# Issuing the causal-mask products of two neighbouring diagonal pieces together, in a fused attention and expert kernel on one Trainium2 core

## What is computed

```python
q_lr = jnp.einsum('bhtd,hdr->bhtr', q, Wq_lsr)
k_lr = jnp.einsum('bhtd,hdr->bhtr', k, Wk_lsr)
scores = jnp.einsum('bhir,bhjr->bhij', q_lr, k_lr) * scale
causal_mask = jnp.triu(jnp.ones((Tq, Tq), dtype=bool), k=1)
scores = jnp.where(causal_mask, jnp.float32(-jnp.inf), scores)
attn = jax.nn.softmax(scores, axis=-1)
y = jnp.einsum('bhij,bhjd->bhid', attn, v)
```

## Time and profile before

| | us |
|---|---|
| median of 3 runs | 4045.71 |
| lowest and highest run | 4045.3, 4045.78 |
| span of the profiled execution | 4045.2 |
| PE busy in it | 3714.7 |
| DVE busy in it | 2261.6 |
| ACT busy in it | 1476.5 |
| attention, from the first slot's first score to the end of the last batch (about) | 147 to 2300 |
| an ordinary slot | 53 to 54 |

### The profile page before, as it was taken

The page is one execution under the profiler, slowest core; times in us unless marked ns, Lnnn a source line. Parts: engine busy times, 40 slices in busy tenths (PEclk is TensorE's granted clock), DMA queues, the critical chain, the costliest instruction groups (busy, mean ns, idle before and its releaser), DMA issues. The chain is left out here.

```text
span 4045.2 us, 57491 instructions
## 1 busy us (share of the span) xinstructions
PE 3714.7 (92%) x21481; PEld 2552.8 (63%) x21481; DVE 2261.6 (56%) x3998; ACT 1476.5 (37%) x2763; POOL 663.2 (16%) x853
## 2 busy tenths in 40 slices
PE   5899999999999999999999815799999999999995
PEld 3555555555555555555555414688888888888884
DVE  2566565665665655656656467444454444445456
ACT  1243443443444434434434301333333333333335
POOL 2022121121121221211211200011111111111113
PEclk7999999999999999999999955799999999999997
DMA  5134234143323342331433100334344343434458
GB/s 163 43 105 130 60 88 123 43 110 101 104 67 90 98 131 59 94 117 43 110 100 74 64 11 6 131 110 126 118 126 129 120 127 107 127 107 130 117 168 310
DMA packets 188920, 423.62 MB, mean 105 GB/s; under 512 B 39840, under 2 KB 42912, under 8 KB 180512
## 3 DMA queue, kind: packets, MB, share of 16 engines
q1 hardware_dynamic: 162032, 367.97, 29.8%
q0 software_dynamic: 14400, 35.14, 4.4%
q10 hardware_dynamic: 12288, 17.83, 1.6%
HBM read 246.75 MB, written 72.38 MB: 79 GB/s over the span
## 5 line engine op out<-in xcount | busy, mean ns | idle before, releaser
L854 DVE TENSOR_REDUCE max_slots<-shared_banks 128x1 f32<-128x512 f32 (+3 forms) x1536 | 768.1, 549 | 394.7 <-PE shared_banks L628 314.9
L800 ACT ACTIVATE probs<-scores_t 128x512 f32<-128x512 f32 (+3 forms) x1536 | 662.4, 498 | 669.4 <-PE scores_t L670 616.7
L1715 PE MATMUL m_ps_h<-m_tokens_t,m_w_parts 128*128 128x512 f32 x3072 | 740.0, 391 | 1.6 <-DVE m_tokens_t L1597 1.6
L1715 PE MATMUL m_ps_y<-m_w_parts,m_hidden_parts 128*128 128x512 f32 x3072 | 737.3, 390 | 0.6
L1715 PEld LDWEIGHTS m_ps_y<-m_w_parts,m_hidden_parts 128*128 128x128 f32 x3072 | 575.4, 188 | 125.8 <-issue 6.3
L1715 PEld LDWEIGHTS m_ps_h<-m_tokens_t,m_w_parts 128*128 128x128 f32 x3072 | 575.6, 188 | 120.2 <-issue 2.0
L625 PE MATMUL shared_banks<-k_operands,q_operands 96*128 96x512 f32 (+3 forms) x1536 | 512.7, 387 | 38.0 <-DVE max_slots L854 15.9
L670 PE MATMUL scores_t<-q_operands,k_operands 128*128 128x512 f32 (+3 forms) x1536 | 515.0, 392 | 27.5 <-ACT probs L800 19.0
L1533 ACT ACTIVATE m_hidden<-m_ps_h,m_b 128x512 f32<-128x512 f32 x256 | 176.6, 690 | 791.5 <-PE m_ps_h L1715 778.3
L530 POOL TENSOR_SCALAR_AFFINE_SELECT probs<-probs 128x256 f32<-128x256 f32 x512 | 218.7, 430 | 1419.0 <-ACT probs L800 1416.2
L625 PEld LDWEIGHTS shared_banks<-k_operands,q_operands 96*128 96x128 f32 x1536 | 294.9, 194 | 220.4 <-issue 140.2
(11 more groups left out here) (219 smaller groups left out, 3178.1 us busy)
## 6 DMA issues: line engine op xcount, KB each, us to landing
m_w_raw<-in_w1T SPq DMA_DIRECT2D x64, 1024.0 KB, 5.1
m_w_raw<-in_w2T SPq DMA_DIRECT2D x64, 1024.0 KB, 8.6
q_operands<-natural SPq DMA_DIRECT2D x384, 128.0 KB, 2.5
k_operands<-natural SPq DMA_DIRECT2D x384, 128.0 KB, 2.5
wqk_group<-scratch_wqk SPq DMA_DIRECT2D x32, 1024.0 KB, 5.2
natural<-in_xT SPq DMA_DIRECT2D x8, 2048.0 KB, 9.3
x_residual<-in_x ACTq DMA_DIRECT2D x64, 256.0 KB, 2.9
scratch_x<-probs SPq DMA_DIRECT2D x64, 256.0 KB, 2.2
```

The costliest lines, as they stand in the source:

```text
L800: act.activation(probs[:, slot_of(k, h // 2), h % 2, c0:HALF], st[:, (HG * k + h) % SCORE_BANKS, c0:HALF], ACT.Exp, scale=SCALE).then_inc( ...
L854: dve.tensor_reduce(mx[:, h, slot:slot + 1], src[:, 0:n], AX.X, ALU.max).then_inc(bank_free[bank], 1)
L1715: mm = pe.matmul(bank, a, b, start=(first and n == 0), stop=(final and n == len(pairs) - 1))
```

## The change

Two things change. When two diagonal pieces stand next to each other in the order, both score products are issued first and then both mask products; each mask product raises its own piece's `bank_full`. And `MAX_AFTER` is rewritten so that the pieces of a slot come in twos and, after parts 18 and 43, in fours; there are no ones and threes left. The count of instructions of each kind stays the same.

```diff
-MAX_AFTER = (0, 0, 0, 0, 0, 0, 0, 0, 0, 2, 2, 1, 1, 0, 3, 0, 0, 0, 3, 0,
+MAX_AFTER = (0, 0, 0, 0, 0, 0, 0, 0, 0, 2, 2, 0, 2, 0, 2, 0, 0, 0, 4, 0,
...
+def masked_pair(item, other):
+    if other[0] != "max" or other[1] != item[1]:
+        return False
+    _, _, it, k0, n = max_steps()[other[2]]
+    return k0 + n == (it + 1) * P
...
-                        if diag:
-                            mm = pe.matmul(out[:, n - P:n], identb[:], mask_q[:], start=False, stop=True)
-                        mm.then_inc(bank_full[bank], 1)
+                        if not diag:
+                            mm.then_inc(bank_full[bank], 1)
+                        elif waiting is None and masked_pair(item, order[pos + 1]):
+                            waiting = (out[:, n - P:n], bank_full[bank])
+                        else:
+                            if waiting is not None:
+                                block, full = waiting
+                                pe.matmul(block, identb[:], mask_q[:], start=False, stop=True).then_inc(full, 1)
+                                waiting = None
+                            pe.matmul(out[:, n - P:n], identb[:], mask_q[:], start=False, stop=True
+                                      ).then_inc(bank_full[bank], 1)
```

More of the change, by code:

```diff
@@ L192 @@
 AHEAD = 2
-MAX_AFTER = (0, 0, 0, 0, 0, 0, 0, 0, 0, 2, 2, 1, 1, 0, 3, 0, 0, 0, 3, 0,
-             2, 0, 3, 1, 0, 0, 2, 0, 1, 2, 0, 1, 2, 1, 2, 0, 0, 2, 1, 1,
-             0, 2, 2, 4, 1, 0, 1, 2, 1, 0, 1, 1, 0, 0, 0, 0, 0, 0, 0, 0)
+MAX_AFTER = (0, 0, 0, 0, 0, 0, 0, 0, 0, 2, 2, 0, 2, 0, 2, 0, 0, 0, 4, 0,
+             2, 0, 2, 2, 0, 0, 2, 0, 0, 2, 0, 2, 2, 0, 2, 0, 0, 2, 2, 0,
+             0, 2, 2, 4, 2, 0, 0, 2, 2, 0, 0, 2, 0, 0, 0, 0, 0, 0, 0, 0)
 PROJ_AFTER = (46, 47, 56, 57)
@@ L576, in run @@
                 nxt = 0 if lead else b * GROUPS + 1
-                for item in order:
+                waiting = None
+                for pos, item in enumerate(order):
                     kind = item[0]
```

## The result

The changed kernel takes 4116.15 us (median of 4 runs, 4111.12 to 4120.04); the kernel before, on the same chip, 4045.74. The ratio is 1.017, with a 95% interval of 1.0156 to 1.0185: slower, by 70 us. The forecast was 4110 with a range of 4086 to 4130. The profiled execution is the longest of the four, 4120.04 us with a span of 4118.3.

What follows compares the result with a forecast made beforehand. PE's own work was taken to bound ordinary slots. 23 of them at 2.5 us (57.5), eight third slots at 0.8 (6.4) and the lead-in (1) add 65 us to 4045.7: 4110 us, range 4086 to 4130.

Steps and rivals of the forecast that it cites:

- The walk: Ordinary slot, piece by piece: eight waits of PE for a bank, about 3.0 us, less 0.5 saved: 2.5 us longer.

## What to carry to other kernels

Where one engine fills a short ring of buffers and another empties it, walk the new order buffer by buffer: the time at which the last write of each lands, the reader's work ahead of it, and the next writer's earliest start. A saving of 0.7 us of issue time in a slot turned into a loss of 2.3, since it held back the release of the buffers; with ten pairs and the pieces spread, 0.35 us of saving came through. Look for the cheaper prize first: moving the pieces away from the waits, with no other edit, was worth 1.1%.

## What the hardware showed

- The granted clock falls to its lower level (1.2 GHz, 0.50) for parts of the third slots, of five in seven before the change and of all seven after it. In the one from 833.1 on it reads 0.50 from 871.1 to 877.8 us, and PE had waited 2.3 us for a bank up to 870.5. A wait of 2.3 us alone does not do it: the pairs with the old table have that wait in the third slot at 818.7, which reads 1.00, while the new table without pairs has a longest wait of 0.9 us for ACT and 0.7 for DVE in its own at 812.7, which reads 0.97. What sets it off stays open.

```profile
818.70:876.30 57.60, 53.99 (x373) 30.93 (x369) 38.38 (x68) 28.20 (x59) 15.41 (x20) 1.00 0.40 111
```

- Short gaps are dear in another way. The walk adds 0.11 us to each wait for the weights that the waiting product has still to load, and meets the measured waits within 0.1 us; without it the short ones would come out a third to a half too small.
